# Vision-tower kernel: Gelu kept in PSUM, the state chain's halves in f16, routing in groups of eight, rows sent in f32, the last stage on two engines

## The reference

```
patches = X.reshape(B, C, 8, 28, 8, 28).transpose(0, 2, 4, 1, 3, 5).reshape(B, 64, 2352)
tokens  = concat([cls, einsum('bpi,hi->bph', patches, W) + b], axis=1) * pos      # (128, 65, 128)
h = tokens
h = h + lstm(layernorm(h))       # gates = xt + h @ W_hh.T; c = f*c + i*g; h = o*tanh(c)
xt = layernorm(h)                # 8320 tokens
probs = softmax(xt @ router_w.T + router_b)          # 16 experts
topk_p, topk_i = top_k(probs, 2)
for each expert e:  y = gelu(xt @ w1[e].T + b1[e]) @ w2[e].T + b2[e];  acc += y * gate_e
h = h + acc
```

## Time and profile before

| | us |
|---|---|
| three runs | 823.87, 826.77, 827.34; median 826.77 |
| the profiled execution, its own time | 828.66 |
| its span (first to last instruction) | 826.7 |
| PE busy / DVE busy / POOL busy / ACT busy | 662.1 / 609.6 / 543.6 / 425.7 |

### The profile page before, as it was taken

How to read it: one execution, slowest core, us unless ns; L and a number is a source line. 1 busy time by engine, 2 the same in 40 slices (tenths; PEclk the granted TensorE clock), 3 DMA queues, 4 the chain that set the end, 5 groups by cost and what they waited for, 6 DMA issues and landing times. The chain is left out here.

```text
span 826.7 us, 25921 instructions
## 1 busy us (share of the span) xinstructions
PE 662.1 (80%) x7853; PEld 617.3 (75%) x7854; DVE 609.6 (74%) x1896; ACT 425.7 (51%) x1206; POOL 543.6 (66%) x653
## 2 busy tenths in 40 slices
PE   3999999999999999999961098888888888888500
PEld 3999999999999999999960077777777777777400
DVE  3689998998988999889975155666666667666478
ACT  3365566555656665566551065555555556655200
POOL 0123567777777777677776548888888888888800
PEclk9899999999999999999985589999999999999755
DMA  8666677777777777778401523323232333232097
GB/s 310 235 236 236 218 250 254 248 229 232 253 256 232 240 259 243 228 240 269 143 27 36 149 77 83 90 83 85 82 88 81 86 85 84 83 91 66 18 331 287
DMA packets 73873, 141.08 MB, mean 171 GB/s; under 512 B 13430, under 2 KB 55874, under 8 KB 65470
## 3 DMA queue, kind: packets, MB, share of 16 engines
q1 hardware_dynamic: 62992, 120.43, 45.6%
q0 software_dynamic: 9280, 17.21, 6.2%
q10 hardware_dynamic: 1518, 2.41, 0.9%
HBM read 116.29 MB, written 25.66 MB: 172 GB/s over the span
## 5 line engine op out<-in xcount | busy, mean ns | idle before, releaser
L952 POOL DMA_INDIRECT back<-patches x160 | 191.1, 1194 | 39.1 <-issue 32.8
L975 PE MATMUL bank<-ws,patches 128*128 128x128 f32 (+1 forms) x1408 | 175.7, 282 | 9.6 <-DMA patches<-in_x 9.6
L924 POOL DMA_INDIRECT sent<-pay,slot_own x130 | 155.7, 1198 | 34.7 <-issue 34.7
L543 ACT ACTIVATE patches<-bank,b1s 128x256 f32<-128x256 f32 x320 | 125.7, 476 | 94.5 <-PE bank L1078 94.5
L975 PEld LDWEIGHTS bank<-ws,patches 128*128 128x128 f32 (+1 forms) x1408 | 166.4, 196 | 9.2 <-ACT whi L451 9.2
L900 POOL TENSOR_TENSOR rstd<-veps,cst 128x2 f32<-128x2 f32 (+1 forms) x68 | 49.1, 722 | 118.3 <-DVE veps L626 117.3
L1078 PE MATMUL bank<-patches,ex_hi 128*128 128x256 f16 x640 | 112.9, 278 | 16.7 <-issue 15.5
L1090 PE MATMUL bank<-ex_hi,patches 128*128 x1280 | 112.6, 220 | 2.9 <-DVE patches L859 2.8
L842 DVE TENSOR_SCALAR patches<-patches 128x2 int32<-128x2 f32 x80 | 20.7, 259 | 114.8 <-DMA back<-patches 97.9
L859 DVE TENSOR_TENSOR patches<-patches 128x1024 f16<-128x1024 f32 x80 | 98.0, 1225 | 2.8
L975 PE MATMUL bank<-whi,xhi 128*128 128x128 f16 x512 | 90.3, 221 | 4.5 <-DVE xlo L661 4.5
(11 more groups left out here) (130 smaller groups left out, 1520.7 us busy)
## 6 DMA issues: line engine op xcount, KB each, us to landing
patches<-in_x SPq DMA_DIRECT2D x64, 1152.0 KB
patches<-sent SPq DMA_DIRECT2D x80, 130.0 KB
patches<-back SPq DMA_DIRECT2D x26, 320.0 KB, 4.9
ex_raw<-in_we SPq DMA_DIRECT2D x64, 128.0 KB
b2r<-in_b SPq DMA_DIRECT2D x80, 64.0 KB, 2.9
posr<-in_pos SPq DMA_DIRECT2D x65, 64.0 KB
out_tower<-h SPq DMA_DIRECT2D x13, 320.0 KB, 4.3
back<-patches POOLq DMA_INDIRECT x160, 2.6
```

The lines of the kernel that those rows point to most:

```text
L543: last = act.activation(hf[n.mod(2)][:, c * ROWS:(c + 1) * ROWS], ps_up(n, c), ACT.Gelu, bias=b1s[:, bass.ds(e * FC + c, 1)], scale=1.0 / ...
L924: pool.indirect_dma_start(sent, bass.IndirectOffsetOnAxis(ap=slot_own[:, g.mod(2), k, col:col + 1], axis=0), pay[:, t.mod(NY), :], None, b ...
L952: pool.indirect_dma_start(back, bass.IndirectOffsetOnAxis(ap=dsti[q][:, k:k + 1], axis=0), yo[q][:, k, :], None, bounds_check=2 * TOKENS - ...
L975: last = pe.matmul(bank_of, l, w_, start=(c == KS and k == 0), stop=(c == KS - 1 and k == 2))
```

## The change

It is spread over all stages.

- **Start.** The first 8 chunks of the weight come by a DMA of their own (`ws_raw`); the first patches are loaded after one memset, not four; the constants are waited for later; the f32 part of `project(2)` is put ahead of the f16 part of `project(1)`.
- **State chain.** The recurrent product is split: `h2_hi` is written straight from the gates, then `h2`, then `h2_lo`; PE does 12 f16 products in place of 4 f32 ones, eight of them before it waits for `h2_lo`. `ca` and `cb` become one operation of 256 columns (`cab`).
- **Rows.** The normalised row is made by ACT in f32 straight into `pay` (scale and `shift2`), so DVE's `yn`, ACT's L507 and POOL's L933 go; `pay` has 24 buffers instead of 8.
- **Routing** works on the logits (`find` and `mask`), in groups of 8 (five), 4 (five), 3 and 2; 16 DVE operations a group and one for the logits. The gates are worked out once at the end. POOL sends by a table `send_slots`.
- **Stage B** is written out without a loop. Gelu goes from PSUM to PSUM in halves; ACT rounds to `hhi`, DVE makes `hlo` from PSUM; PE makes two f32 transposes and DVE splits them; DVE makes the row numbers in one operation; `yo` and `dsti` have 8 buffers.
- **Last stage.** One DMA a step, rows of `back` interleaved; ACT scales the second expert's row, DVE adds five times and then once for 640 columns.

```diff
-U = 8
-UG = 4
-NY = 8
-PACK, SEND = 5, 10
+UG = 8
+SIZES = [8] * 5 + [4] * 5 + [3, 2]
+NP = 24
+NO = 8
...
+        def starting(g):
+            return STARTS[g + 1] - 1 + 3
+        def ready(g):
+            return starting(g) + (2 if quick(g) else 4)
+        def send_slots():
+            slots, n, room = {}, 0, 0
+            for t in range(T):
+                first = ready(place(t)[0]) + 1
+                if first > n:
+                    n, room = first, 1
+                if room == 0:
+                    n, room = n + 1, (2 if n % 2 else 1) if t >= STARTS[4] else 1
+                slots.setdefault(n, []).append(t)
+                room -= 1
+            return slots
...
-            sp.wait_ge(ones_in, NX)
-            load_patches(At(None, 1, U))
+            sp.wait_ge(ones_in, 1)
+            load_patches(1)
... (PE, recurrent product)
-                        through(pe, h_done, n - 1)
+                        through(pe, h_hi_done, n - 1)
+                    here = ps_gate[n % 2]
                     for g in range(4):
-                        last = pe.matmul(ps_gate[n.mod(2)][:, g * B:(g + 1) * B], whh[:, g, :],
-                                         h2[:, (n - 1).mod(2), :], start=False, stop=True, skip_group_check=True)
+                        for w_ in (whh_hi, whh_lo):
+                            pe.matmul(here[:, g * B:(g + 1) * B], w_[:, g, :], h2_hi[:, (n - 1) % 2, :],
+                                      start=False, stop=False, skip_group_check=True)
+                    if n >= 1:
+                        through(pe, h_lo_done, n - 1)
+                    for g in range(4):
+                        last = pe.matmul(here[:, g * B:(g + 1) * B], whh_hi[:, g, :], h2_lo[:, (n - 1) % 2, :],
+                                         start=False, stop=True, skip_group_check=True)
... (DVE, stage B)
+            def remainder(n, half):
+                dve.wait_ge(hhi_done, 2 * n + half + 1)
+                cols = slice(half * 512, (half + 1) * 512)
+                dve.tensor_tensor(hlo[n % 4][:, cols], ps_up(n, half)[:, :], hhi[n % 4][:, cols],
+                                  ALU.subtract).then_inc(hlo_done, 1)
...
+                    dve.scalar_tensor_tensor(dsti[n % NO], xt[n % 4][:, :, HID + 1], tabj[:, 0, n:n + 1],
+                                             xt[n % 4][:, :, HID], ALU.not_equal, ALU.add).then_inc(dst_done, 1)
... (ACT, stage B)
+            def gelu(n, half, e):
+                act.wait_ge(up_ps, 2 * n + half + 1)
+                up = ps_up(n, half)
+                for i in range(2):
+                    cols = slice(i * ROWS, (i + 1) * ROWS)
+                    last = act.activation(up[:, cols], up[:, cols], ACT.Gelu,
+                                          bias=b1s[:, bass.ds(e * FC + 2 * half + i, 1)], scale=1.0 / E_SCALE)
+                last.then_inc(gelu_done, 1)
+            def round_off(n, half):
+                act.wait_ge(gelu_done, 2 * n + half + 1)
+                if n >= 4:
+                    through(act, down_ps, n - 4)
+                act.activation(hhi[n % 4][:, half * 512:(half + 1) * 512], ps_up(n, half)[:, :],
+                               ACT.Copy).then_inc(hhi_done, 1)
+            def step_b(n):
+                if 0 <= n <= TILES_B - 1:
+                    e = act.value_load(tabi[0:1, 0, n:n + 1], min_val=0, max_val=E - 1)
+                    gelu(n, 0, e)
+                if 0 <= n - 1 <= TILES_B - 1:
+                    round_off(n - 1, 1)
+                if 0 <= n <= TILES_B - 1:
+                    gelu(n, 1, e)
+                    round_off(n, 0)
... (POOL, stage B)
+            for n in range(TILES_B):
+                through(pool, dst_done, n)
+                through(pool, y_done, n)
+                for k in range(HALVES):
+                    pool.indirect_dma_start(back, bass.IndirectOffsetOnAxis(ap=dsti[n % NO][:, k:k + 1], axis=0),
+                                            yo[n % NO][:, k, :], None, bounds_check=2 * TOKENS - 1,
+                                            oob_is_err=False).then_inc(y_out[n % NO], 16)
... (DVE, last stage; ACT scales bk[q][:, 2 * i + 1, :])
+                    ins = dve.scalar_tensor_tensor(h1[:, t, :], bk[q][:, 2 * i, :], gates[:, 0, t:t + 1],
+                                                   h1[:, t, :], ALU.mult, ALU.add)
+                ins.then_inc(add_a, 1)
+                through(dve, add_a, m)
+                through(dve, scaled_second, m)
+                here = h1[:, m * CT:(m + 1) * CT, :]
+                dve.tensor_tensor(here, here, bk[q].rearrange("p (i k) h -> p i k h", k=2)[:, :, 1, :],
+                                  ALU.add).then_inc(add_b, 1)
```

More of the change, by code:

```diff
@@ L273, in tower @@
+        STARTS = np.cumsum([0] + SIZES).tolist()
         LAST_SLOT = T - 1 + 6
-        def slots(eng, step, width, first, start, high, last):
-            bodies = (high + 1 - start) // width
-            for n in range(first, start):
-                step(At(None, n, width))
-            with eng.Fori(0, bodies) as i:
-                for n in range(start, start + width):
-                    step(At(i, n, width))
-            for n in range(start + bodies * width, last + 1):
-                step(At(None, n, width))
@@ L390, in _ @@
                 sp.dma_start(rows_of(sent, row), pad[:, :, :]).then_inc(pads_sp, 16)
-            for t in range(T - NY, T):
-                rows_sent(sp, At(None, t, U))
+            for t in range(T - NP, T):
+                rows_sent(sp, t)
             sp.wait_ge(pads_sp, 16 * E // 2)
@@ new lines, in step @@
+                if halved:
+                    split(t, KS // 2, KS).then_inc(hi_done, 1)
+                if n == -3:
+                    recurrent_weights()
+                t = n - 1
+                if 0 <= t <= T - 1:
+                    through(act, shift_done, t)
+                    if t >= NP:
+                        rows_sent(act, t - NP)
+                    act.activation(pay[:, t % NP, 0:HID], h1[:, t, :], ACT.Identity, bias=shift2[:, t % 2:t % 2 + 1],
+                                   scale=rstd[:, 1:2]).then_inc(yn_done, 1)
@@ new lines, in _ @@
+            slots_b(act, step_b)
+            act.wait_ge(under, 2)
+            act.activation(lg[:, :, :], lg[:, :, :], ACT.Exp)
+            act.activation(top[:, 1, :], top[:, 1, :], ACT.Exp).then_inc(exp_done, 1)
+            for m in range(T // CT):
+                q = m % NX
+                act.wait_ge(bk_in[q], 16 * (m // NX + 1))
+                if m == 0:
+                    act.wait_ge(gate_done, 3)
+                for i in range(CT):
+                    t = m * CT + i
+                    last = act.activation(bk[q][:, 2 * i + 1, :], bk[q][:, 2 * i + 1, :], ACT.Identity,
+                                          scale=gates[:, 1, t:t + 1])
+                last.then_inc(scaled_second, 1)
@@ L668, in _ @@
+                for g in range(GROUPS):
+                    pieces = (route_first, route_first_mask, route_second, route_second_mask)
+                    if quick(g) and 0 <= n - starting(g) <= 1:
+                        for route in pieces[2 * (n - starting(g)):2 * (n - starting(g)) + 2]:
+                            route(g, STARTS[g], SIZES[g])
+                    elif not quick(g) and 0 <= n - starting(g) <= 3:
+                        pieces[n - starting(g)](g, STARTS[g], SIZES[g])
             class Group:
```

840 lines of the change are left out of this document (393 added, 447 removed).

## The result

| | changed | before, beside it |
|---|---|---|
| median of four runs | 754.21 us (750.86 to 756.3) | 825.61 us (823.87 to 827.34) |
| ratio | 0.913, 95% interval 0.909 to 0.918 | |
| the profiled execution | 750.86, span 749.0 | 828.66, span 826.7 |

The change saves 71 us. The time lies inside the range of 705 to 772, but 23 us above the forecast of 731, and outside the band of 718 to 745 that had a chance of 0.50. Of the 23, 5 come from which executions were profiled (the changed one is 3.4 under its median; for the one before the forecast took off 1.9, the distance to the median of its three runs), and 18 are the sum's: it said 95.7 us less where the two profiled executions differ by 77.8.

The account below looks back on a forecast made before the run. Bounds: PE and DVE near 6 us a slot in stage A, a four-buffer loop with the write-back's landing in stage B. Savings 6 + 18 + 15 + 52 + 2.7 + 2 = 95.7 from 828.7, less 1.9: 731 us, range 705 to 772.

Parts of the forecast that it names:

- Start: Before stage A: second f32 projection moved into PE's hole and first patches asked for earlier; 6 us saved, bounds 0 and 8.
- Slots: Stage A's 64 slots: each falls from 6.25 to 5.97 us, 18 us saved, bounds 0 and 37.
- I take 5.97: Stage A: slot time chosen above the computed mean of 5.89, for POOL's double sends and the expert piece's DMA.
- the rival with 0.15: Stage A: slots stay at 6.25 as DVE's chain, expert-piece DMA and double sends eat PE's 0.30; 749 us, chance 0.15.
- the missing 0.28 us is DVE's: Stage A before the change: slots take 6.25 against PE's 5.97 without waits; the difference was put down to DVE.
- DVE needs 5.9 in the middle ones: Stage A: DVE's time in slots with routing of eight tokens, with 6.3 in one and PE's 5.67 in three.
- Tail: From stage A's last recurrent product to stage B's first transpose: 46 us becomes 31, 15 saved, bounds 8 and 20.
- Now six are left at slot 64: Tail of stage A: six tokens left for POOL to send instead of ten, its sends ending 3 us before the padding.
- Stage B: Eight buffers take the landing out of the loop, PE bounds; tile 3.71 to 3.05 us, 52 us saved, bounds 17 and 66.
- Behind the last result: After stage B's last result: 2.7 us as POOL no longer runs two tiles late, plus 2 us in the last stage.
- The other side: Stage B: DVE's new PSUM operations hold sends to 1.93 us, tile 4.46, 842 us; the two slower cases together 0.04.
- the rivals on the slots and on ACT: Slots stay at 6.25: 749 us, chance 0.15. ACT bounds stage B at 3.5 us a tile: 767 us, chance 0.20.

## Why the prediction was right in its range and wrong in its parts

- **Start:** 4.5 for 6. In the kernel before, PE's wait in the hole (4.53 us) ended with `xlo` on DVE, not with a landing of weights; the hole was there all the same. The second f32 projection now starts at 16.78, but waits 2.3 us for its patches to land. That was the reason given for the lower bound.
- **Slots:** -0.5 for 18. The step that failed is "I take 5.97". PE's 5.67 was right (5.68), and DVE's fixed part, at 5.1, too high rather than too low. The 5.97 was DVE's 5.89 and 0.08 a slot, 5 us in all, for the landing and the doubled sends together, with no working for it; and the 5.89 left out the small groups. The runs show two parts. The first is the expert piece's DMA, which lands 6.2 us after its issue; the earlier trace rows showed the waits, and the prediction named it in the rival with 0.15. It was to be weighed as a bound: what follows ACT's 25 waits (the gates, in order on the same engine) is on PE's chain, and an engine that gets faster meets the same landing. Even the sentence "the missing 0.28 us is DVE's" was mostly the landing: 0.20. Asking for the piece one slot earlier gives back 16.8 us of slots in the changed kernel and 12.5 in the one before, and of the miss 6 us in the first 46 slots are its share. The second, 12.6 us of the miss, is the last 18 slots. There the step "DVE needs 5.9 in the middle ones" used the groups of eight for all 64 slots: spreading the small groups gave back 6 us. And the doubled sends, which the prediction named, hold DVE by up to 1.9 us: some 5 us. Both are read with the piece early; no run spread the groups with the piece late.
- **Tail:** 7.3 for 15. "Now six are left at slot 64" is wrong: nine tokens follow, and 18 sends end 3.4 us behind the padding, where I had them 3 us ahead of it. The chain on DVE that I added up is not the last to end, and it has a wait for POOL (4.4 us) that I did not see.
- **Stage B:** 62.6 for 52. The mechanism is as said: with four buffers the landing is back (3.47), and with eight PE is the bound. The term was mis-sized by the 0.18 of waits that I added to PE's floor of 2.87: it measured 0.035, and 0.145 over 79 tiles is the 10.6. ACT had 2.5 of 2.9 us to do, as worked out, and the register load hides.
- **Behind the last result:** 3.8 for 4.7. In the last stage the DMA share is 1.02 at 417 GB/s with ACT waiting 0.8 us a step for the load, so its bound is the transfer, as forecast.
- **The other side:** DVE's new operations read PSUM, and none of them held a send. One of the 160 was held, by an operation for the gates with two SBUF inputs (L889, shown below). It was rightly given little.

In sum, four terms too large by 28.6 us in all were set off by one too small by 10.6. That they set each other off is luck; without stage B's 10.6 the time would be 765, still inside the range, which held because it took in the rivals on the slots and on ACT. The rival on the slots (749) comes nearest, in time and in mechanism; it had the tail too short by 7.7 and stage B too slow by 10.6, as the forecast had.

## What to carry to other kernels

Work out a gain for each part of a stage, not for its mean slot: here the first 46 slots gained and the last 18 lost. When two engines are close to the bound, a wait for a DMA on a third one counts as a bound of its own, if what is queued behind it in order feeds the chain: compare the time from issue to landing with the period, and ask for the data one period earlier before shortening the period. Work that is spread evenly must stay so for the short groups at the end too, for one lump of 2 us costs 4 when PE's clock falls behind it. A loop over buffers with a landing in it can be cured by more buffers: eight for four gave 0.5 of the 0.8 us a tile.

## What the runs showed of the hardware

- **A send begun under a DVE subtraction with two SBUF inputs** ends 0.84 us after the subtraction's end (685.04 and 684.20 above; in the earlier trace rows 640.94 and 640.08, so 0.86), and alone it takes 0.97. So it waits for the end and then does nearly all its work. In the kernel before, 26 of the 160 sends begin so and take 1.68 to 2.20 us. The one held send of the changed kernel stands under another `tensor_tensor` of that kind, and ends 0.85 us after it (588.71 and 587.86):

```profile
586.63 1.23 DVE L889 TENSOR_TENSOR lg<-lg,top 128x1040 f32<-128x1040 f32 x1
586.70 2.01 POOL L970 DMA_INDIRECT back<-patches  x1 [0.30 <-issue]
```

The Trainium skill ("SBUF — State Buffer", A bandwidth-pool intuition that's wrong) describes such a wait until DVE's end for a DMA beside a `tensor_copy` that holds the shared port. The same form shows here for a `tensor_tensor`, with its own numbers.
- **PE's clock after a gap:** 0.63 on average over 4.6 us behind a stretch in which PE was busy for 0.29 of 2.0 us; the projection then takes 3.94 for 2.67 us.
- **Two kinds of chips.** The changed kernel takes 754 us on one and 845 on the other, the kernel before 826 and 858. Most of the changed kernel's 91 us is stage B: (800.3 - 493.6) / 79 = 3.88 us a tile. PE in one tile there:

```profile
599.96 0.28 PE L1107 MATMUL bank<-patches,ex_hi 128*128 128x256 f16 x1
600.81 0.27 PE L1107 MATMUL bank<-patches,ex_hi 128*128 128x256 f16 x1 [0.57 <-issue]
601.54 0.27 PE L1107 MATMUL bank<-patches,ex_lo 128*128 128x256 f16 x1 [0.46 <-issue]
602.27 0.38 PE L1107 MATMUL bank<-patches,ex_hi 128*128 128x256 f16 x2 [0.46 <-issue]
```

Matmuls that follow at 0.11 on the first kind come at 0.85, 0.73 and 0.73 there, with nothing shown that they wait for; from 500 to 700 us the waits of this line on "issue" come to 25.5 us in 41 times, and the changed kernel on the first kind has none. All five kernels that ran on the second kind have such tiles (3.88 to 3.94). Why PE's queue pauses there is open; no run tried to tell. The kernel before, whose stage B waits for POOL and the landing, is 32 us slower on that kind; the changed one, whose stage B has PE as its bound, 91.
